# Top-k pattern layers of a hybrid network: counting moved from VectorE to ScalarE, bracket arithmetic to GpSimd, tile pairs in four lanes

## What is computed

```python
input_acts = gelu(x @ input_patterns.T)                    # 1024 per token
input_repr = input_acts where it is in its row's top 128, else 0
process_acts = gelu(input_repr @ process_input_weights.T)  # 512 per token
p_weights = softmax(the row's top 64 of process_acts)
agg_value = p_weights @ process_values                     # 128 per token
output_acts = gelu(agg_value @ output_input_weights.T)     # 1024 per token
out = (output_acts where in the row's top 128, else 0) @ output_patterns
```

## Time and profile before

| what | us |
| --- | --- |
| runs of this kernel | 5950.46, 5954.21, 6311.34 |
| their median | 5954.21 |
| the profiled execution's own time | 5961.62 |
| its span, first to last instruction | 5959.8 |
| pattern stage, first to last instruction in it (2565.70 to 3986.10) | 1420.4 |

### The profile page before, as it was taken

One profiled execution on the slowest core, in us unless ns is written; L12 is line 12 of the kernel. 1 busy time (PEld: TensorE's weight loads), 2 busy tenths in 40 slices (PEclk: granted clock), 3 DMA queues, 4 the chain that ended last, 5 costly groups with the idle time before them and its releaser, 6 DMA issues. The chain is left out here.

```text
span 5959.8 us, 144342 instructions
## 1 busy us (share of the span) xinstructions
PE 4680.3 (79%) x57740; PEld 2937.0 (49%) x57741; DVE 3653.8 (61%) x10008; ACT 1932.3 (32%) x3675; POOL 485.6 (8%) x940
## 2 busy tenths in 40 slices
PE   3778888989798889845555655558999999997796
PEld 1257777734377777513333333324544454554564
DVE  3445444530254554459999999965868687884343
ACT  1133322311233332111121112114757576671221
POOL 0000000000000000000000000001111111110312
PEclk7878888979888898877777777778999999997897
DMA  1000000000000000000000000000000000003323
GB/s 38 2 7 3 3 3 3 3 16 0 6 3 3 3 3 3 4 34 1 0 0 0 0 0 0 0 1 9 0 1 0 1 0 1 1 0 122 118 79 100
DMA packets 47569, 85.79 MB, mean 14 GB/s; under 512 B 7120, under 2 KB 38128, under 8 KB 46064
## 3 DMA queue, kind: packets, MB, share of 16 engines
q1 hardware_dynamic: 40944, 61.84, 3.1%
q0 software_dynamic: 6144, 16.79, 0.9%
HBM read 45.05 MB, written 33.55 MB: 13 GB/s over the span
## 5 line engine op out<-in xcount | busy, mean ns | idle before, releaser
L1761 PE MATMUL psum<-hm_ex,hm_mix 128*128 128x512 f32 x1024 | 510.6, 621 | 42.2 <-ACT hm_Aq L1841 38.2
L1334 DVE TENSOR_SCALAR_CACHE_REDUCE pt_over<-pt_acts,pt_tb 128x1024 f32<-128x1024 f32 (+1 forms) x416 | 446.3, 1111 | 0.0
L1184 PE MATMUL psum<-K,pt_kept 128*128 128x128 f32 x512 | 96.2, 350 | 372.6 <-DVE pt_kept L1390 372.6
L1827 ACT ACTIVATE hm_ex<-psum,hm_nm 128x1024 f32<-128x1024 f32 x256 | 285.5, 1115 | 296.2 <-DVE hm_nm L1885 296.0
L1761 PEld LDWEIGHTS psum<-hm_ex,hm_mix 128*128 128x128 f32 x1024 | 175.6, 191 | 350.9 <-issue 343.2
L1900 DVE COPY hm_A<-psum 128x1024 f32<-128x1024 f32 x256 | 312.9, 1222 | 51.8 <-PE psum L1770 48.0
L1895 DVE TENSOR_SCALAR_CACHE_REDUCE hm_plus<-hm_Aq,hm_cbcol,hm_sums 128x1024 f32<-128x1024 f32 x256 | 340.4, 1330 | 0.0
L957 DVE TENSOR_TENSOR fw_M<-fw_M,psum 128x256 f32<-128x256 f32 x256 | 107.9, 421 | 345.2 <-PE psum L728 340.1
L1885 DVE TENSOR_REDUCE hm_nm<-psum 128x1 f32<-128x1024 f32 x256 | 311.0, 1215 | 12.1 <-PE psum L1749 12.1
L1770 PEld LDWEIGHTS psum<-K,hm_Aq 128*128 128x128 f32 x2048 | 236.6, 140 | 150.1 <-issue 145.3
L1195 PE MATMUL psum<-pt_w_proc,pt_keptT 128*128 128x512 f32 x512 | 265.5, 678 | 37.2 <-ACT pt_keptT L1263 37.2
(11 more groups left out here) (380 smaller groups left out, 9332.8 us busy)
## 6 DMA issues: line engine op xcount, KB each, us to landing
ex_rows_in<-ex_zero SPq DMA_DIRECT2D x2, 5120.0 KB, 24.5
ex_xs<-ex_rows_in SPq DMA_DIRECT2D x80, 128.0 KB, 2.1
ex_rows_out<-ex_ys SPq DMA_DIRECT2D x80, 128.0 KB, 1.7
ex_w<-in_ex_w SPq DMA_DIRECT2D x2, 4096.0 KB, 21.6
X<-in_x SPq DMA_DIRECT2D x2, 2048.0 KB, 12.6
out_y<-X SPq DMA_DIRECT2D x2, 2048.0 KB, 9.0
ff_w<-in_ff_w SPq DMA_DIRECT2D x2, 1024.0 KB, 5.9
pt_w_proc<-in_pt_proc SPq DMA_DIRECT2D x1, 2048.0 KB, 9.6
```

What stands on the lines that cost most here:

```text
L1334: both(lambda u: dve.tensor_scalar(over[:, u, 0:n], a(u), trial(u), 0.5 - keep, ALU.is_ge, ALU.add, accum_out=off(u)))
L1761: mm = pe.matmul(bank[4 + c], mix[:, u, :], ex[:, u, 512 * c:512 * c + 512], start=True, stop=True)
L1827: act.activation(ex[:, u, :], flat2(psum[:, 2 * u:2 * u + 2, :]), ACT.Exp, bias=nm[:, u:u + 1], accum_out=rsum[:, u:u + 1]).then_inc(s_ex, 1)
```

## The change

The stage's source is rewritten; the other stages stay. The work is cut into 48 jobs: a job is one layer of one pair of tiles. Four pairs are in flight, in four lanes, and jobs 0 to 3 are the first layer of lanes 0 to 3, jobs 4 to 7 the second, 8 to 11 the third, then the next four pairs. The loop is written out as 52 slots, s = -1 to 50. In slot s, TensorE turns and multiplies the kept rows of job s-3 and so makes the scores of job s+1; ScalarE copies, applies Gelu to the scores of job s+1, and counts for jobs s and s-1; GpSimd narrows the brackets of those two; VectorE closes job s-2. A slot is called an input, process or output slot by the layer of job s-3; these are s = 3 to 6, 7 to 10 and 11 to 14, and so on in twelves.

What moves: all but the last count go to ScalarE, as a Sign pass with the trial as bias and the row's sum (3, 3 and 4 of them per job); the narrowing goes to GpSimd, 11 instructions for both tiles together, with a power of -1 for the reciprocal; the last count and the closing stay on VectorE, their small instructions now for both tiles at once. The kept row is written over the activations, scores are made from `H` directly, and ScalarE writes the result into `H`. Weights arrive behind `w_in`, for which alone the first matmul waits. `start` and `num` are rescaled to sums of signs.

```diff
     nc, d = k.nc, k.d
     FAR = 2.0 ** 100
     N_IN, N_PROC, N_OUT, D_PV = 1024, 512, 1024, 128
-    IN, PROC, OUT = (N_IN, 128, 4, 0), (N_PROC, 64, 4, 1), (N_OUT, 128, 5, 2)
+    LAYERS = ((N_IN, 128, 3), (N_PROC, 64, 3), (N_OUT, 128, 4))
+    LANES = 4
+    NJ = 3 * NT // 2
+    layer = lambda j: j % 12 // 4
+    lane = lambda j: j % LANES
+    tile = lambda j, u: 2 * (LANES * (j // 12) + lane(j)) + u
...
+        def turned(s):
+            return layer(s - 3) if s >= 3 else FIRST
+
+        def makes(s):
+
+            return s + 1 < NJ
+
+        def counting(s):
+
+            return [(j, c) for j, c in ((s, 0), (s - 1, 2), (s, 1), (s - 1, 3))
+                    if 0 <= j < NJ and c < LAYERS[layer(j)][2]]
...
+                sp.wait_ge(s_w, 16)
+                for to, n in ((w_proc, "pt_proc"), (w_val, "pt_val"), (w_out, "pt_out")):
                     sp.dma_start(to[:, :, :], d[n]).then_inc(s_w, 16)
-                sp.dma_start(start[:, :, :, :], d["pt_start"]).then_inc(s_w, 16)
                 sp.dma_start(w_oi[:, :], d["pt_oi"]).then_inc(s_w, 16)
...
+                def begin(j):
+                    pool.wait_ge(s_g, n_act(j - 1, 1))
+                    n = lane(j)
+                    own.done(pool.tensor_tensor(
+                        first[:, :, :], start[:, layer(j), 0, :].unsqueeze(1).broadcast_to([P, 2, 6]),
+                        total[:, n, :].unsqueeze(2).broadcast_to([P, 2, 6]), ALU.mult))
+                    pool.tensor_tensor(tb[:, n, :, :], first[:, :, :],
+                                       start[:, layer(j), 1, :].unsqueeze(1).broadcast_to([P, 2, 6]),
+                                       ALU.add).then_inc(s_begun, 1)
+
+                def narrow(j, c):
+
+
+                    l, n = layer(j), lane(j)
+                    bracket = tb[:, n, :, 2:6].rearrange("p u (b v) -> p u b v", b=2)
+                    pool.wait_ge(s_cnt, 2 * n_count[j, c])
+                    own.mark(pool.tensor_scalar(above[:, :, 0:1], tb[:, n, :, 1:2], float(middle(l)), None, ALU.is_gt))
+                    own.mark(pool.tensor_scalar(above[:, :, 1:2], tb[:, n, :, 1:2], float(middle(l)), None, ALU.is_lt))
+                    own.done(pool.tensor_tensor(db[:, :, :, :], tb[:, n, :, 0:2].unsqueeze(2).broadcast_to([P, 2, 2, 2]),
+                                                bracket, ALU.subtract))
+                    own.done(pool.tensor_tensor(db[:, :, :, :], db[:, :, :, :],
+                                                above[:, :, :].unsqueeze(3).broadcast_to([P, 2, 2, 2]), ALU.mult))
+                    own.done(pool.tensor_tensor(bracket, bracket, db[:, :, :, :], ALU.add))
+                    own.mark(pool.tensor_tensor(df[:, :, :], tb[:, n, :, 2:4], tb[:, n, :, 4:6], ALU.subtract))
+                    own.done(pool.tensor_scalar(rest[:, :], tb[:, n, :, 3], -float(middle(l)), None, ALU.add))
+                    own.mark(pool.tensor_tensor(slope[:, :], df[:, :, 1], minus[:, :], ALU.pow))
+                    own.done(pool.tensor_tensor(rest[:, :], rest[:, :], df[:, :, 0], ALU.mult))
+                    own.done(pool.tensor_tensor(rest[:, :], rest[:, :], slope[:, :], ALU.mult))
+                    ends = (tb[:, n, :, 2], rest[:, :])
+                    if c + 1 == LAYERS[l][2]:
+                        ends = ends[::-1]
...
+                for s in SLOTS:
+                    if 0 <= s < NJ:
+                        begin(s)
+                    for j, c in counting(s):
+                        narrow(j, c)
...
+                def to_process(s):
+                    j = s - 3
+                    if lane(j) == 0 and j >= 12:
+                        pe.wait_ge(s_yc, n_of_layer(j - 1, 1))
+                    turn(s, 0, 2, N_IN // P)
+                    pe.wait_ge(s_g, n_act(s - 1, 0))
+                    turn(s, 1, 0, N_IN // P)
                     for u in range(2):
-                        turn(v, u, job + u)
-                        pe.wait_ge(s_gp, 4 * i + v + u + 1)
+                        pe.wait_ge(s_g, n_act(s - 1, u if turned(s - 1) == IN else 1))
+                        pe.wait_ge(s_tc, n_turn(s, u))
                         for c in range(N_IN // P):
-                            mm = pe.matmul(bank[4], keptT[:, u, c, :], w_proc[:, c, :], start=(c == 0),
...
+                def count(s, at):
+                    if at >= len(counting(s)):
+                        return
+                    j, c = counting(s)[at]
+                    n = LAYERS[layer(j)][0]
+                    if c == 0:
+                        act.wait_ge(s_begun, j + 1)
+                    else:
+                        act.wait_ge(s_trial, n_count[j, c - 1])
                     for u in range(2):
-                        turned(u, job + u)
-                        gelu(v, u, N_PROC, bank[4], s_p, 4 * i + v + u + 1, s_gp)
-
-                def after_process(i, v, last):
+                        if n_count[j, c] > 1:
+                            act.wait_ge(s_cnt, 2 * n_count[j, c] - 3 + u)
+                        act.activation(signs[:, u, 0:n], acts[:, lane(j), u, 0:n], ACT.Sign,
+                                       bias=tb[:, lane(j), u, 0:1],
...
+                        count(s, 0)
+                        gelu(s, 0)
+                        count(s, 1)
+                        gelu(s, 1)
+                        weights(s)
+                        count(s, 2)
+                        count(s, 3)
+                    elif turned(s) == IN:
+                        turned_copy(s, 0)
+                        turned_copy(s, 1)
+                        weights(s)
+                        count(s, 0)
+                        count(s, 1)
+                        gelu(s, 0)
+                        count(s, 2)
+                        count(s, 3)
+                        gelu(s, 1)
+                    elif turned(s) == PROC:
+                        turned_copy(s, 0)
+                        turned_copy(s, 1)
+                        aggregated(s, 0)
+                        aggregated(s, 1)
+                        weights(s)
+                        count(s, 0)
+                        gelu(s, 0)
+                        count(s, 1)
+                        gelu(s, 1)
+                        count(s, 2)
+                        count(s, 3)
+                    else:
+                        turned_copy(s, 0)
+                        weights(s)
+                        count(s, 0)
+                        gelu(s, 0)
+                        turned_copy(s, 1)
+                        count(s, 1)
+                        gelu(s, 1)
+                        count(s, 2)
+                        result(s, 0)
+                        count(s, 3)
+                        result(s, 1)
 
             @block.vector
             def _(dve):
-                own = (Steps(dve, s_dch0), Steps(dve, s_dch1))
...
+                def close(j):
+                    n, keep, counts = LAYERS[layer(j)]
+                    a = lambda u: acts[:, lane(j), u, 0:n]
+                    if layer(j) == PROC:
+                        dve.wait_ge(s_g, n_act(j - 1, 1))
+                        for u in range(2):
+                            dve.tensor_reduce(top[:, u:u + 1], a(u), AX.X, ALU.max, negate=True).then_inc(s_top, 1)
+                    dve.wait_ge(s_trial, n_count[j, counts - 1])
                     for u in range(2):
-                        own[u].sync()
...
+                        own.mark(dve.tensor_scalar(over[:, u, 0:n], a(u), tb[:, lane(j), u, 0:1], 0.5 - keep, ALU.is_ge,
+                                                   ALU.add, accum_out=off[:, u:u + 1]))
+                    own.sync()
+                    own.done(dve.tensor_scalar(half[:, :], off[:, :], 0.0, -0.5, ALU.is_lt, ALU.add))
+                    own.mark(dve.tensor_scalar(gain[:, :], half[:, :], -2.0 * FAR, None, ALU.mult))
+                    own.mark(dve.tensor_scalar(shift[:, :], half[:, :], -0.5, FAR, ALU.add, ALU.mult))
+                    own.done(dve.tensor_tensor(at[:, :], off[:, :], half[:, :], ALU.mult))
+                    own.mark(dve.tensor_scalar(at[:, :], at[:, :], -2.0, -0.5, ALU.mult, ALU.add))
...
+                        own.mark(dve.tensor_scalar(over[:, u, 0:n], over[:, u, 0:n], gain[:, u:u + 1], shift[:, u:u + 1],
+                                                   ALU.mult, ALU.add))
+                    own.sync()
...
+                        own.mark(dve.scalar_tensor_tensor(side[:, u, 0:n], a(u), half[:, u:u + 1], over[:, u, 0:n],
+                                                          ALU.mult, ALU.add))
+                    own.mark(dve.tensor_tensor(mine[:, :, :], num[:, 0, :].unsqueeze(1).broadcast_to([P, 2, 8]),
+                                               at[:, :].unsqueeze(2).broadcast_to([P, 2, 8]), ALU.is_equal))
+                    own.sync()
...
+                        own.mark(dve.max(best[:, u, :], side[:, u, 0:n]))
```

(13 more changed lines are left out.)

399 lines of the change are left out of this document (144 added, 255 removed).

## The result

The changed kernel takes 5414.5 us at the median of 4 runs, the kernel before, beside it, 5970.8: a ratio of 0.908, 95% interval 0.902 to 0.914. The ratio leaves out one run of the kernel before, 6311.3 us, which stood in a slower state of the chip and is still in the median of 5970.8. The forecast was 5405 us, the range 5330 to 5600. The profiled execution took 5396.8 us.

What follows compares the result with a forecast made beforehand. VectorE was taken to bound the pattern stage; with work moved off it, 54 + 3 x 208.5 + 137 + 54 = 870 us instead of 1420.4, so 5961.6 becomes 5412, forecast as a median of 5405 us, range 5330 to 5600.

Steps and rivals of the forecast that it cites:

- The input slots: Pattern stage, first-layer products: TensorE at full clock sets 16.1 us a slot, 64 us for four.
- The process slots: Pattern stage, second-layer products: ScalarE's work in order, unhidden by TensorE, takes 16.0, 17.6, 20.8 and 17.1 us, sum 71.5.
- The output slots: Pattern stage, third-layer products and new scores: TensorE sets 16.6 us a slot, 66 for four, plus 2 at half clock.
- GpSimd: Narrowings at 2.9 us: twelve slots need 171 us, 49 lost beside VectorE's passes; under the others' 203.5, 5 added for waits.
- VectorE's close: VectorE's closing of a wide pair takes 13.3 us, so twelve slots need at most 160 us, where before 340.
- Twelve slots: One full group of input, process and output slots: 132 + 71.5 + 5 = 208.5 us, against 340 before.
- Eight slots more: The input and process slots after three groups of twelve, up to slot 46: 64 + 71.5 + 2 = 137 us.
- Lead: Ahead of slot 3: first load, scores and Gelu, counts and narrowings, a close and waits, 54 us.
- Tail: Behind slot 46: three closes of 13.3 less 1.2, then 15.7 from first transpose to the end, 54 us.
- GpSimd as the bound: GpSimd decides from 3.8 us per narrowing; at 5.4, stage 1102 and total 5636 us, still faster; chance 0.15.
- The sums of signs: Rival: Sign-based counts leave some row unsure and the search stage runs, some 2800 us more; chance 0.02.
- Rival 3: TensorE stays at half clock throughout: twelve slots 334 us, stage 1318, total 5852, within 2%; chance 0.03.

Runs made afterwards that it cites:

- e5: Changed kernel with two further 512-column matmuls ahead of each tile's product in the 16 input slots; stage 923.2 us, 57.6 more.
- e2: Changed kernel with a further pair of wide Sign passes on ScalarE in each of the 16 process slots; stage 892.9 us.
- e6: Changed kernel with the power in each GpSimd narrowing made a multiplication; stage 840.2 us, 25 less; whole kernel 9786 us, as the search stage runs.
- e7: Changed kernel with VectorE's two-input passes of the close made one-input passes, in the process layer only the first; stage 830.2 us, 35 less.
- e9: Changed kernel with the last narrowing of each tile pair done by VectorE right before the close, instead of by GpSimd; stage 831.1 us.
- e10: Changed kernel with each pair's last narrowing on VectorE and the next pair's begin ahead of GpSimd's later narrowings; stage 827.3 us, 0.901 of the kernel before.
- e11: Changed kernel's unrolled order and four lanes, but VectorE counts, narrows and closes, with no searching on ScalarE or GpSimd; stage 1329.1 us.
- e4: Changed kernel with two more dependent small operations on GpSimd in each of the 160 narrowings; stage 916.5 us, 51 more.

## Why the prediction was right, by its own steps

The stage was forecast at 870 us and is 870.6; but that the sum is right to 1 us is luck, since terms missed in both directions.

- **The input slots** (16.1 each, 64 for four): 64.0 to 64.7, clock 1.00. Shown by e5.
- **The process slots** (71.5, all ScalarE): 69.7. The mechanism is right for three of them (e2), the sizes were off. The first is 13.2 for 16.0: its aggregates are done 3.0 us into the slot and not 5.1, since TensorE comes right from an input slot (the sixteen rows of L1233 take 2.05 us there, 3.66 in the next slot), and halves of Signs are 0.71 without a gap for the read. The last is 20.2 for 17.1, and 4.3 of that are waits for GpSimd, which the term did not have.
- **The Sign pair** (2.4, half 1.6): 2.27 and 1.4.
- **The output slots** (66, and 2 for the first one's start at half clock): 73.8 to 75.6. This is the step that failed. "ScalarE needs 11 to 15.5 us and TensorE hides it" is true of its work but not of its waits: in the first two slots the chain from count to trial to count, with blocked narrowings and the begin behind them, takes 20 us. e6, e7, e9 and e10 each take part of it away, and e10 comes to 65.
- **GpSimd** (171 us of twelve slots, 49 of them blocked, and 5 us of waits on the path): an unhindered narrowing is 3.05 us for 2.9, with the unknown power at 0.72. Its durations sum to 2.76 and a begin's to 0.41, so twelve slots without hindrance would be busy 40 x 2.76 + 12 x 0.41 = 115 us; busy are 148.5, so 33 were lost, not 49. The sum was well under 208, as said. But I let a chain cost only what its sum exceeds, plus "four slots of twelve about 1.2". By e10 against the changed kernel it costs 11 us in twelve slots, not 5.
- **VectorE's close** (13.3): 13.45 between the starts of two parts in e10 (2780.17 to 2793.62); 149 us busy in twelve slots for at most 160. It is no bound.
- **Twelve slots** (208.5): 208.1, 209.3, 207.7. Output slots 6 to 8 too long, process slots 1.8 too long a forecast, and the 5 for waits make up for each other.
- **Eight slots more** (137; the terms given there add up to 137.5): 133.5, since the process slots are shorter than forecast.
- **Lead** (54): 51.1, from the load to slot 3's first copy. **Tail** (54): 60.9; in the last output slots, too, Signs wait for GpSimd (3.3, 3.0, 2.3 and 2.5 us), and TensorE then for kept rows.
- **What was costed at nothing:** the written-out loop and the place of the rows starve no engine; e11, which has both, is 76 us shorter than before.
- **The rivals:** GpSimd as the bound needed 3.8 us per narrowing; e4, with 0.54 more in each, is at 3.6 and already pays 0.6 of what is added. It was near. Half clock fell with 1.00 in the input slots. The sums of signs left no row unsure: the search stage does not run. Rival 3's stage of 1318 should be some 1312 by its own terms, which moves nothing.
- **The median** (5405): 5414.5.

## What to carry to other kernels

When work moves from one engine to three, look for the bound slot by slot: here busy shares of 66 to 78% hid three different limits. A chain between two engines costs by its latency and by what is queued behind it: GpSimd was busy 71% of twelve slots, and in two of them it had no gap but the 2.5 us of its own loop; a small step whose only reader is the engine that does the next big one belongs there, even where that engine is the busier one. And the length of a wait is not its price: 70 us of waits went for 12 us of time, while elsewhere the same waits stayed and 26 us went.

## What the runs showed of the hardware

- Eleven small dependent operations take 3.05 us on GpSimd and 1.54 on VectorE. An operation of 128x2 is 0.19 to 0.22 us on the one, with 0.27 from start to start where the result is waited for, and 0.16 to 0.17 on the other, with 0.20.
- A power of 128x2 on GpSimd takes 0.72 us, nearly four times a multiplication (0.20), in 160 cases never under 0.718.
- A GpSimd operation of 0.20 us is held for one pass of VectorE each time, 1.09 to 1.25 us beside two-input passes, also beside one-input passes at double rate (0.59 to 0.72 us), and not beside counting passes (0.20 to 0.22).
- Sign with a sum over 1024 columns in SBUF is 1.14 us, over 512 0.71, back to back with the sum's read inside; the table loads of the stage are, as before, 16 for the exponential and 17 for the Gelu, and Sign adds none.
